# A windowed-attention and feed-forward kernel: each query-key product issued as two of 64 columns, and its loops written out

## The reference, cut to what matters

```python
q, k, v = jnp.split(x @ w_qkv, 3, axis=-1)            # 16 heads of 64
sim = jnp.einsum('bhnid,bhnjd->bhnij', qw, kw)        # block n: queries i, window keys j
sim = jnp.where(mask[None, None], mask_value, sim)
attn = stable_softmax(sim, axis=-1)
attn = jnp.einsum('gh,bhnij->bgnij', w_th, attn)      # the heads are mixed
out = jnp.einsum('bhnij,bhnjd->bhnid', attn, vw)
x = _layernorm(x + (out @ w_out + b_out), axis=-1)
h = gelu(_ternary_linear(x, w_up)); x = _layernorm(x + _ternary_linear(h, w_down), axis=-1)
```

## Time and profile before

| what | us |
|---|---|
| median of 3 runs | 308.44 |
| the profiled execution's own time | 311.5 |
| its span, first to last instruction | 309.6 |
| PE matmul busy | 263.1 |
| VectorE busy | 179.8 |
| ScalarE busy | 156.8 |
| GpSimd busy | 67.1 |
| one full attention step (145.04 to 151.14) | 6.10 |
| one step without Y (215.38 to 220.12) | 4.74 |

### The profile page before, as it was taken

How to read it: one execution, slowest core, us unless ns; L and a number is a source line. 1 busy time by engine, 2 the same in 40 slices (tenths; PEclk the granted TensorE clock), 3 DMA queues, 4 the chain that set the end, 5 groups by cost and what they waited for, 6 DMA issues and landing times.

```text
span 309.6 us, 6860 instructions
## 1 busy us (share of the span) xinstructions
PE 263.1 (85%) x2176; PEld 243.0 (78%) x2176; DVE 179.8 (58%) x408; ACT 156.8 (51%) x298; POOL 67.1 (22%) x120
## 2 busy tenths in 40 slices
PE   0458989999999999999999999999996968687440
PEld 0448889999999999999999999999995946565320
DVE  0333822687666466556655665665876467865721
ACT  1263731566545554554545464644453099777500
POOL 6050010211211211111121112111220436655320
PEclk9987996999999999999999999999999899787755
DMA  4658697000700600510330240060000000010011
GB/s 124 191 169 299 190 181 98 4 2 2 106 2 0 103 3 0 90 16 0 67 39 0 46 60 0 20 86 0 0 0 0 0 4 0 0 34 29 5 34 34
DMA packets 18481, 15.78 MB, mean 51 GB/s; under 512 B 1568, under 2 KB 17828, under 8 KB 18340
## 3 DMA queue, kind: packets, MB, share of 16 engines
q1 hardware_dynamic: 18468, 15.62, 23.7%
HBM read 11.28 MB, written 4.33 MB: 50 GB/s over the span
## 4 chain that ended last, share of the span: by engine, by line
PE 78%; DVE 7%; ACT 4%; issue 3%; DMA 2%; SPq 2%; DVEq 1%; POOL 0%; ACTq 0%; POOLq 0%
PE bank L942 18%; PE bank L816 10%; PE bank L817 10%; PE bank L818 10%; PE bank L910 9%; PE bank L897 6%; DMA xq<-in_L_attn_x 2%; PE bank L1023 2%; PE bank L1024 2%; PE bank L856 2%; PE bank L1009 1%; PE bank L862 1%; DVE CTl L660 1%; DVE st L762 1%; DVE y L757 1%
## 5 line engine op out<-in xcount | busy, mean ns | idle before, releaser
L660 DVE TENSOR_TENSOR CTl<-bank,CTh 128x512 fp32r<-128x512 f32 x64 | 41.2, 686 | 42.4 <-ACT CTh L434 42.2
L434 ACT ACTIVATE Yb<-bank 128x512 f32<-128x512 f32 x64 | 37.8, 590 | 52.8 <-PE bank L818 52.3
L377 POOL TENSOR_TENSOR E<-E,rc 128x400 f32<-128x400 f32 x32 | 27.4, 857 | 168.1 <-DVE rc L690 168.1
L942 PE MATMUL bank<-xT,Yb 128*128 x512 | 62.1, 276 | 0.8 <-ACT Yb L434 0.8
L942 PEld LDWEIGHTS bank<-xT,Yb 128*128 128x128 f32 x512 | 61.3, 196 | 1.0 <-issue 1.0
L434 ACT ACTIVATE CTh<-bank 128x512 fp32r<-128x512 f32 x64 | 34.7, 595 | 32.3 <-PE bank L910 32.3
L816 PE MATMUL bank<-xTh,Gh 128*128 (+1 forms) x128 | 39.4, 308 | 0.6 <-DVE Gl L612 0.5
L816 PE MATMUL bank<-CTh,Mh 128*128 128x256 f32 x128 | 37.0, 289 | 1.4 <-DVE CTl L660 1.4
L817 PE MATMUL bank<-xTl,Gh 128*128 (+1 forms) x128 | 36.3, 283 | 0.0
L818 PE MATMUL bank<-xTh,Gl 128*128 (+1 forms) x128 | 36.3, 283 | 0.0
L817 PE MATMUL bank<-CTl,Mh 128*128 128x256 f32 x128 | 36.1, 282 | 0.0
(11 more groups left out here) (122 smaller groups left out, 430.1 us busy)
## 6 DMA issues: line engine op xcount, KB each, us to landing
xw<-x_rows SPq DMA_DIRECT2D x48, 128.0 KB
x_rows<-xs SPq DMA_DIRECT2D x4, 512.0 KB
w_sb<-in_L_attn_w_qkv SPq DMA_DIRECT2D x3, 512.0 KB, 7.1
pt_rows<-PT SPq DMA_DIRECT2D x1, 1024.0 KB, 6.2
R<-pt_rows SPq DMA_DIRECT2D x1, 1024.0 KB, 5.3
xq<-in_L_attn_x SPq DMA_DIRECT2D x2, 448.0 KB
out<-outS SPq DMA_DIRECT2D x4, 192.0 KB
wo_sb<-in_L_attn_w_out SPq DMA_DIRECT2D x1, 512.0 KB, 6.3
```

What stands on the lines that cost most here:

```text
L377: nc.gpsimd.tensor_tensor(e, e, rc[j % 2][:, :].unsqueeze(2).broadcast_to([P, TILES, WIN]), ALU.mult).then_inc(s_norm, 1)
L434: copy = lambda o, i, **k: nc.scalar.activation(o, i, ACT.Copy, **k)
L660: v.tensor_tensor(ct_view(CTl[par], sc, bk), c_view(bk), ct_view(f32(CTh[par][:, :, :]), sc, bk), ALU.subtract).then_inc(s_CTl, 1)
L942: mm(bank[S_BANK[k]][:, WIN * tile:WIN * tile + WIN], Yb[(j // 4) % 2][:, ytile, :], keys, start=(tile == 0), stop=False, skip_group_check ...
```

## The change: two products of 64 columns for one of 128, and loops as text

Each query-key product is issued twice, with 64 of the 128 stationary columns each (`rows`) and the same 50 keys. The first writes partitions 0 to 63 of the bank, the second 64 to 127; in the built program such a product has a tile of 128 rows by 64 columns of the array, at column 0 or 64. The two halves of a tile are issued one behind the other. All hardware loops become Python loops, all conditions are settled at build time, and indices are constants.

```diff
-        def since(eng, I, j, d):
-
-            return nullcontext() if j >= d else eng.If(I > 0)
...
+        def since(I, j, d):
+
+            return j >= d or I > 0
...
+        def ds(first, n):
+
+            return slice(first, first + n)
...
-            with act.Fori(0, ITERS) as g:
+            for g in range(ITERS):
...
-            with dve.Fori(0, ITERS) as g:
+            for g in range(ITERS):
...
-            with pe.Fori(0, ITERS) as I:
+            for I in range(ITERS):
                 for j in range(SLOTS):
...
-                        keys = xT17[:, bass.ds(I, 1), :, :].rearrange("p i u s -> p (i u s)")[:, SEG * blk:SEG * blk + WIN]
-                        mm(bank[S_BANK[k]][:, WIN * tile:WIN * tile + WIN], Yb[(j // 4) % 2][:, ytile, :], keys,
-                           start=(tile == 0), stop=False, skip_group_check=True)
+                        keys = xT17[:, ds(I, 1), :, :].rearrange("p i u s -> p (i u s)")[:, SEG * blk:SEG * blk + WIN]
+                        for rows in (slice(0, 64), slice(64, 128)):
+                            mm(bank[S_BANK[k]][rows, WIN * tile:WIN * tile + WIN], Yb[(j // 4) % 2][:, ytile, rows], keys,
+                               start=(tile == 0), stop=False, skip_group_check=True)
```

More of the change, by code:

```diff
@@ L20 @@
 from concourse import mybir
-from contextlib import ExitStack, nullcontext
+from contextlib import ExitStack
 F32 = mybir.dt.float32
@@ L236, in attention_ffn, with before_last @@
         AHEAD_STORE = 16 * STORES
-        def since(eng, I, j, d):
-            return nullcontext() if j >= d else eng.If(I > 0)
-        def before_last(eng, I, j):
-            return nullcontext() if j < SLOTS // 2 else eng.If(I < ITERS - 1)
+        def since(I, j, d):
+            return j >= d or I > 0
+        def before_last(I, j):
+            return j < SLOTS // 2 or I < ITERS - 1
+        def ds(first, n):
+            return slice(first, first + n)
         def heads(i):
@@ L305, in _ @@
             sp.wait_ge(s_xrows, 16 * XROW_DMAS)
-            with sp.Fori(0, ITERS) as I:
+            for I in range(ITERS):
                 for par in range(2):
@@ L323, in _ @@
             sp.sem_inc(f_store, AHEAD_STORE)
-            with sp.Fori(0, B) as b:
+            for b in range(B):
                 for half in range(2):
@@ L372, in _ @@
             pool.sem_inc(s_norm, AHEAD_NORM)
-            with pool.Fori(0, ITERS) as I:
+            for I in range(ITERS):
                 for j in range(SLOTS):
@@ L422, in _ @@
             up_scale(0)
-            with pool.Fori(0, ITERS + 1) as g:
-                with pool.If(g > 0):
+            for g in range(ITERS + 1):
+                if g > 0:
                     down_scale(g)
-                with pool.If(g < ITERS - 1):
+                if g < ITERS - 1:
                     scale(g + 1)
                     up_scale(g + 1)
-                with pool.If(g > 0):
+                if g > 0:
                     scale2(g)
@@ L482, in _ @@
             act.sem_inc(s_Oe, AHEAD_OE)
-            with act.Fori(0, ITERS) as I:
+            for I in range(ITERS):
                 for j in range(SLOTS):
@@ L488, in _ @@
                         act.wait_ge(s_O, AHEAD_O + 2 * I)
-                    with since(act, I, j, LAG + 1):
+                    if since(I, j, LAG + 1):
                         ct_hi(j, 16 * I + 2 * (j - LAG - 1))
-                    with since(act, I, j, LAG):
+                    if since(I, j, LAG):
                         at_hi(j, SLOTS * I + j + 1 - LAG)
                     def y_out(b):
-                        with before_last(act, I, j):
+                        if before_last(I, j):
                             if j % 4 == 0 and b == 0:
@@ L566, in _ @@
                 squares(g, 0)
-                with act.If(g > 0):
+                if g > 0:
                     down_out(g)
@@ L576, in _ @@
                 h_hi(g, 2)
-                with act.If(g < ITERS - 1):
+                if g < ITERS - 1:
                     x1_hi(g + 1)
@@ L670, in _ @@
             dve.sem_inc(s_ATl, AHEAD_ATL)
-            with dve.Fori(0, ITERS) as I:
+            for I in range(ITERS):
                 for j in range(SLOTS):
                     k = j % 2
-                    with since(dve, I, j, LAG + 1):
+                    if since(I, j, LAG + 1):
                         ct_lo(j, 16 * I + 2 * (j - LAG - 1))
-                    with since(dve, I, j, LAG):
+                    if since(I, j, LAG):
                         at_lo(j, SLOTS * I + j + 1 - LAG)
@@ L691, in _ @@
                     if j < len(IN_STEP):
-                        with dve.If(I < 1):
+                        if I < 1:
                             fills(IN_STEP[j])
@@ L747, in keep @@
                 dve.wait_ge(f_x1, 4 * g + 4)
-                v.tensor_copy(x1keep[:, bass.ds(g % 2 * TPI, TPI), :], x1[:, :, :]).then_inc(f_x1c, 1)
+                v.tensor_copy(x1keep[:, ds(g % 2 * TPI, TPI), :], x1[:, :, :]).then_inc(f_x1c, 1)
             def second(g):
@@ L788, in _ @@
             bos_row(1, 2 * ITERS)
-            with dve.Fori(0, ITERS) as g:
+            for g in range(ITERS):
                 keep(g)
-                with dve.If(g < ITERS - 1):
+                if g < ITERS - 1:
                     residual(g + 1)
-                with dve.If(g < ITERS - 2):
+                if g < ITERS - 2:
                     stage(g + 2)
                 h_lo(g, 0)
-                with dve.If(g < ITERS - 1):
+                if g < ITERS - 1:
                     layernorm(g + 1)
                 h_lo(g, 1)
-                with dve.If(g > 0):
+                if g > 0:
                     second(g)
-                with dve.If(g < ITERS - 1):
+                if g < ITERS - 1:
                     x1_lo(g + 1)
@@ L926, in _ @@
             pe.sem_inc(s_O, AHEAD_O)
-            with pe.Fori(0, ITERS) as I:
+            for I in range(ITERS):
                 for j in range(SLOTS):
                     k = j % 2
-                    with since(pe, I, j, LAG):
+                    if since(I, j, LAG):
                         pe.wait_ge(s_ATl, AHEAD_ATL + SLOTS * I + j - LAG)
@@ L954, in _ @@
                     ins.then_inc(s_S, 1)
-                    with before_last(pe, I, j):
+                    if before_last(I, j):
                         for b in range(2):
                             pe.wait_ge(s_Ye, 16 * I + 2 * j + b + 7)
-                            y_part(b, bass.ds((2 * I + j // 4 + 1) % (2 * ITERS) * CHUNK, CHUNK), 4 * (j % 4) + 2 * b)
+                            y_part(b, ds((2 * I + j // 4 + 1) % (2 * ITERS) * CHUNK, CHUNK), 4 * (j % 4) + 2 * b)
                     if j < len(IN_STEP):
-                        with pe.If(I < 1):
+                        if I < 1:
                             fills(IN_STEP[j])
@@ L968, in _ @@
                         pe.wait_ge(s_evd, read_no("D", "m", 3))
-                    with since(pe, I, j, 4 + LAG):
+                    if since(I, j, 4 + LAG):
                         n, p = divmod(j + 4 - LAG, 4)
@@ L1049, in _ @@
             up(0, 1)
-            with pe.Fori(0, ITERS) as g:
+            for g in range(ITERS):
                 h_T(g, 0)
                 up(g, 2)
-                with pe.If(g > 0):
+                if g > 0:
                     down_back(g)
@@ L1057, in _ @@
                 h_T(g, 2)
-                with pe.If(g < ITERS - 1):
+                if g < ITERS - 1:
                     x1_T(g + 1)
                 h_T(g, 3)
-                with pe.If(g < ITERS - 1):
+                if g < ITERS - 1:
                     pe.wait_ge(f_xTl, g + 2)
@@ L1064, in _ @@
                     up(g + 1, 1)
-                with pe.If(g < ITERS - 2):
+                if g < ITERS - 2:
                     attn_back(g + 2)
```

24 lines of the change are left out of this document (12 added, 12 removed).

## The result

The changed kernel took 291.79 us, the median of four runs (288.91 to 294.07), beside 308.78 for the kernel before: a ratio of 0.9369, 95% interval 0.9299 to 0.9439. Measured again with the experiments it was 290.86 us beside 311.52 on that chip, 0.9326 (0.9264 to 0.9387). Forecast was 293.0, a ratio of 0.950: the direction and the mechanism came as forecast. By the medians the kernel gained 17.0 us in the first measurement and 20.7 in the second, by the ratios 19.5 and 20.8; forecast were 15.4.

The account below looks back on a forecast made before the run. TensorE alone was taken to bound the attention. The split's 13.4 us and the loops' 2.0 came off the profiled 311.5 (296.1); the same 15.4 off the median 308.44 gave 293.0. Range for 8 in 10: 289 to 320.

Parts of the forecast that it names:

- TensorE alone sets the time, and weight loads set the 1.72 us: Attention loop: TensorE is the bound; a step's 16 query-key records cost 0.108 us each, set by loading 128 columns.
- at full clock from the third slice on: Profile page's clock slices: TensorE was read as at full clock from the third slice to the attention's end.
- Pairs at 0.058: Query-key products: two 64-column halves go together, 0.058 us a pair, so a step's 16 pairs take 0.93 us.
- the 1.2 to 1.4 that were to show it: Sign that the forecast is right: the 32 query-key records of a step take 1.2 to 1.4 us.
- Edges of 0.36: Each attention step: one more round trip between full and tiled array costs 0.36 us, from 0 to double.
- Five short steps held by VectorE's slack of 0.35: Five steps with only Y or only O: VectorE's slack before `ct_lo` limits each one's gain to 0.35 us.
- Fetches cost nothing: Attention loop: instruction fetches for the longer straight program charged at nothing; 30 us if TensorE waited for each added packet.
- Loops 2.0: Attention and feed-forward loops written out: table loads, registers and branches saved give 2.0 us, from 0.5 to 5.
- Clock: Behind the attention: slow-clock stretches after idle cost about 2 us; change counted as 0, with 2 either way.
- the clock 1.00 throughout the attention: Sign that the forecast is right: TensorE's granted clock stays at 1.00 for the whole attention.
- loads in turn: Query-key halves' 32 loads go singly at 0.056 us: 320.2 us in all; chance 0.25, shared with pairs of unshortened loads.
- Streams in turn: Query-key halves: loads pair but key streams go singly, 32 at 0.043 us; 307.0 us in all; chance 0.10.

Follow-up runs that it names:

- quarters: The changed kernel with each query-key product issued in four of 32 stationary columns instead of two of 64; 285.41 us, ratio 0.9095.

## Why the prediction was right, step by step

*TensorE alone sets the time, and weight loads set the 1.72 us.* Right: the step fell with the loads, and halves in an order without pairs, with the same loads at 0.057 each, were as slow as whole ones (1.81 us). One reading beside it was wrong: TensorE is not at full clock from the third slice on. The third, fourth and seventh slice have 8, 7 and 6 tenths, and the seventh is the second attention step.

*Pairs at 0.058.* Right: 15 distances in 0.87 us, and 1.07 us from the first record to the mask, a little under the 1.2 to 1.4 that were to show it. What the row tiles of `c_part` showed held for column tiles, on the same rows of the memory and with the same keys read twice.

*Edges of 0.36.* The term that was mis-sized. From the timelines above: 0.09 at the entry (0.58 against 0.49), and 1.07 - 0.93 = 0.14 for the first pair and the exit, 0.23 together. The 0.36 was 0.21 for `c_part` and 0.15 for the transposes behind it. The 0.15 is 0.59 - 0.44, with 0.59 from the chain of waits; by the starts of the timeline before (144.39 and 144.88) the transposes take 0.49, which leaves 0.05, and 0.26 for the round trip. Full steps fell by 0.52 us in the mean instead of 0.43. Over the 25 behind the second that is 2.2 us, about half of the 4.6 by which the two profiled spans differ more than forecast (20.0 against 15.4); 1.2 more lie in the preparation and 0.6 in the first two steps, where the clock differs between executions. One more slip is on record: without edges the sum would be 9.7 us lower (27 x 0.36), not 11, since the five short steps were held to 0.35 anyway.

*Five short steps held by VectorE's slack of 0.35.* Wrong in cause; that the sum came out is luck. The four distances that start at a short step and end at another step's first record were 4.73, 4.74, 4.75 and 4.74 and are 4.18, 4.20, 4.20 and 4.91. Three gave 0.55, the last gave nothing and lost 0.17: 1.47 in all, where 4 x 0.35 = 1.4 were forecast (the fifth short step has none behind it). VectorE's cycle did give up its 0.35 in front of `ct_lo` and went to 4.28, but TensorE's steps went below it, to 4.20, and a VectorE with 0.2 us less work didn't change them. What cost time is the latency from `c_part` to `o_part` at one place, and that wait wasn't among the rivals.

*Fetches cost nothing.* Right: the queue has 21 packets instead of 7, 29 with quarters, and TensorE's only idle time between the first and the last query-key record is the 0.57 us in front of `o_part`.

```profile
q8 instruction: 21, 0.34, 0.6%
```

*Loops 2.0.* Right within the interval of 1.6 to 4.2. One table load is left in the feed-forward part, as forecast; what the other three were worth can't be told from the rest.

*Clock.* Counted as 0, with 2 either way, behind the attention only. It is the largest disturbance between single executions, 4 us, and it acts in the preparation and in the first two attention steps too, which the prediction had left out. Its sign "the clock 1.00 throughout the attention" failed there, before and after.

Of the rivals, loads in turn is what the order with halves apart makes of the kernel, and it gave 312 where 320 had been forecast for it; by the 6.29 us of its steps, again the edges. By the rule of the Trainium skill, "TensorE: Matmul & The Clock Gate", section "The mechanism", that a load overlaps a running matmul only with another row group, the halves should have gone so in the changed kernel too. The trace disagrees: two loads of the same row groups start within 0.015 us, and in a full step loads are busy for 5.07 of 5.55 us beside a matmul row that is busy throughout. (In the prediction's count of loads beside matmuls in the same rows, `c_part`'s 12 a step don't belong: their neighbours are in other rows.) Streams in turn are excluded already by the halves (32 at 0.043 would be 1.38 us, and took 1.07), and clearly by the quarters: 64 would be 2.8 us, and took 0.85.

## What to carry to other kernels

Where products have few moving columns, as the 50 here, the weight load is the price, and it goes by stationary columns: try the stationary operand in column halves or quarters that follow each other in the order. Halves took this piece from 1.72 to 1.07 us, quarters to 0.85. Issue the tiles of one array mode together: one change of mode less gave 0.2 us in a full step here (5.55 to 5.35). And look at the steps that lack the usual filler work: a chain of copies that was hidden comes out there when TensorE gets faster. Before a gain in one stage is read from two profiles, compare the granted clock of the others.

## What the runs showed of the hardware that was not expected

The order in the program decides the pairing: with 16 records of one half ahead of 16 of the other, 32 took 1.81 us, with the halves alternating by product 1.07. Four quarters go together as well, 64 products in 0.85 us. A change of array mode and back cost about 0.23 us, worked out from the pieces above. And one kernel's preparation lasted 39.4 or 43.4 us, with the same 32 products at 2.79 us (granted clock 1.00) or 5.10 (0.50).
